# First attention: order of ScalarE's exponentials and copies, and which engine writes the upper halves of queries and keys

## The reference, cut to what matters

```
x = layernorm(x)
q, k, v = x @ Wq, x @ Wk, x @ Wv          # 16 heads of 64 columns
scores  = (q / 8) @ k.T, causal mask
attn    = softmax(scores)
out     = (attn @ v) @ Wo + bo
```

## Time and profile before

| | us |
|---|---|
| median of 3 runs | 3022.37 |
| lowest and highest run | 3019.58, 3025.27 |
| the profiled execution | 3037.7 |
| its span, first to last instruction | 3035.6 |

### The profile page before, as it was taken

The page is one execution under the profiler, slowest core; times in us unless marked ns, Lnnn a source line. Parts: engine busy times, 40 slices in busy tenths (PEclk is TensorE's granted clock), DMA queues, the critical chain, the costliest instruction groups (busy, mean ns, idle before and its releaser), DMA issues.

```text
span 3035.6 us, 54384 instructions
## 1 busy us (share of the span) xinstructions
PE 2616.6 (86%) x20224; PEld 1702.2 (56%) x20224; DVE 2026.0 (67%) x4632; ACT 1685.6 (56%) x3282; POOL 900.1 (30%) x931
## 2 busy tenths in 40 slices
PE   7999999999999999588898558787875969999979
PEld 4666766676667667564446436666765532333325
DVE  5565566556655654257875246999998868888845
ACT  4767566656666665241222227868874436677762
POOL 1000011001100110452232465767876212322221
PEclk9999999999999999799999788898988979999999
DMA  5000000000000001120001111121221540100000
GB/s 184 2 2 2 1 6 6 2 2 6 6 2 2 7 5 42 43 64 14 8 10 54 51 47 49 64 70 64 76 72 56 200 139 2 58 30 30 2 2 29
DMA packets 79941, 114.22 MB, mean 38 GB/s; under 512 B 10109, under 2 KB 48172, under 8 KB 79680
## 3 DMA queue, kind: packets, MB, share of 16 engines
q1 hardware_dynamic: 71488, 97.07, 9.8%
q0 software_dynamic: 8192, 13.67, 1.6%
HBM read 77.66 MB, written 35.78 MB: 37 GB/s over the span
## 4 chain that ended last, share of the span: by engine, by line
PE 27%; issue 13%; POOL 9%; DVE 5%; another core or an unknown queue 3%; ACT 3%; DMA 1%; SPq 0%; POOLq 0%; ACTq 0%; DVEq 0%
POOL arena L2094 7%; PE ps L2323 4%; PE ps L1202 3%; PE ps L1396 3%; PE ps L2294 2%; PE ps L2281 2%; PE ps L2285 2%; ACT arena L2403 2%; PE ps L696 1%; PE ps L1405 1%; PE ps L685 1%; PE ps L1193 1%; DVE Wqkv L2444 1%; POOL arena L993 1%
## 5 line engine op out<-in xcount | busy, mean ns | idle before, releaser
L387 ACT ACTIVATE arena<-ps 128x512 f32<-128x512 f32 (+1 forms) x640 | 334.6, 548 | 376.0 <-PE ps L291 356.2
L499 DVE CUSTOM_DVE_ANT_0 arena<-ps,causal 128x512 f32<-128x512 f32 (+3 forms) x512 | 282.4, 589 | 302.0 <-PE ps L278 266.6
L400 ACT ACTIVATE arena<-arena 128x640 f32<-128x640 f32 (+7 forms) x512 | 394.1, 770 | 37.9 <-DVE arena L499 33.5
L2444 DVE TENSOR_REDUCE Wqkv<-ps 128x2 f32<-128x1024 f32 (+2 forms) x320 | 345.3, 1114 | 87.9 <-PE ps L2285 60.5
L291 PE MATMUL ps<-ident,arena 128*128 128x128 f32 x2304 | 345.9, 282 | 47.6 <-ACT arena L400 30.3
L2094 POOL TENSOR_TENSOR arena<-arena,W 128x1024 f32<-128x1024 f32 x128 | 332.5, 2617 | 134.0 <-DVE W L2046 134.0
L2403 ACT ACTIVATE arena<-ps 128x1024 f32<-128x1024 f32 (+1 forms) x320 | 291.8, 939 | 134.2 <-PE ps L2294 131.2
L1802 PE MATMUL ps<-rope,arena 128*128 128x128 f32 x2048 | 282.6, 300 | 96.2 <-DVE W L2032 47.3
L291 PEld LDWEIGHTS ps<-ident,arena 128*128 128x128 f32 x2304 | 252.0, 142 | 167.7 <-issue 91.2
L577 POOL COPY arena<-arena 128x512 f32<-128x512 f32 x64 | 39.3, 613 | 1027.5 <-DVE arena L523 635.7
L1802 PEld LDWEIGHTS ps<-rope,arena 128*128 128x128 f32 x2048 | 268.2, 213 | 126.3 <-issue 69.1
(11 more groups left out here) (265 smaller groups left out, 4258.4 us busy)
## 6 DMA issues: line engine op xcount, KB each, us to landing
select<-c_rows SPq DMA_DIRECT2D x64, 512.0 KB, 3.6
arena<-q_dram SPq DMA_DIRECT2D x4, 2048.0 KB, 8.9
arena<-k_dram SPq DMA_DIRECT2D x4, 2048.0 KB, 14.0
q_dram<-arena SPq DMA_DIRECT2D x24, 256.0 KB, 3.7
k_dram<-arena SPq DMA_DIRECT2D x24, 256.0 KB, 3.7
arena<-slots_in SPq DMA_DIRECT2D x8, 640.0 KB, 6.7
slots_out<-arena SPq DMA_DIRECT2D x8, 640.0 KB, 4.3
slots_in<-select SPq DMA_DIRECT2D x4, 640.0 KB, 6.4
```

The source lines that it names most:

```text
L387: nc.scalar.activation(k.probT[:, n % 2, b0 * P:(b0 + nb) * P], k.ps[:, 4 + m % 2, 0:nb * P], ACT.Copy)\
L400: nc.scalar.activation(k.prob[:, i % 2, h, 0:w], k.prob[:, i % 2, h, 0:w], ACT.Exp, bias=k.neg_max[:, i % 2, h:h + 1], scale=-1.0, accum_o ...
L499: ins = nc.vector.tensor_tensor_reduce(k.prob[:, i % 2, h, 512 * g:512 * g + w], k.ps[:, banks[h], 0:w], k.causal[:, first:first + w], 1.0 ...
L2444: nc.vector.tensor_reduce(k.least[:, g, As[0]:As[-1] + 1, i % 4, c, :], k.ps[:, 2 * slot:2 * slot + 2, 0:len(As) * w].rearrange("p h (a w) ...
```

## The change

`upper` moves from VectorE's program to ScalarE's. There it stands in steps 0 and 1 of every pair that has a next one (`ahead`), as one activation (Copy with a scale) for each half of 512 columns, waiting for the projection (`qk_ps`) and telling `hi` as before. In steps 0, 1 and 2 of such pairs both exponentials of the step now stand in front of all copies of the step, and in steps 0 and 1 the upper halves stand between the exponentials and the copies. Steps 3 to 7 and the last pair keep their order.

```diff
@@ act_attention_a, pair
+        def upper(w, banks):
+            act.wait_ge(sm["qk_ps"], p * 2 + w + 3)
+            for g in range(2):
+                nc.scalar.activation((k.q_parts, k.k_parts)[w][:, 1 - parity, 0, g * 512:(g + 1) * 512], k.ps[:, banks[g], :],
+                                     ACT.Copy, scale=QK_SCALE[w]).then_inc(sm["hi"], 1)
+
...
             inverse = r is not None and u % 4 == 3
+            if ahead and i < 3:
+                exponential(i, 0)
+                exponential(i, 1)
+            if ahead and i < 2:
+                upper(i, a_banks("project", p, i))
             early = (len(pieces) + inverse + 1) // 2
             for m, b0, nb in pieces[:early]:
                 copy(q, n, m, b0, nb)
             if inverse and early > len(pieces):
                 take_inverse(r, u // 4)
-            if i < 8:
+            if i < 8 and not (ahead and i < 3):
                 exponential(i, 0)
             for m, b0, nb in pieces[early:]:
                 copy(q, n, m, b0, nb)
             if inverse and early <= len(pieces):
                 take_inverse(r, u // 4)
-            if i < 8:
+            if i < 8 and not (ahead and i < 3):
                 exponential(i, 1)
@@ dve_attention_a, pair
-        def upper(w, banks):
-            dve.wait_ge(sm["qk_ps"], p * 2 + w + 3)
-            for g in range(2):
-                nc.vector.tensor_scalar((k.q_parts, k.k_parts)[w][:, 1 - parity, 0, g * 512:(g + 1) * 512],
-                                        k.ps[:, banks[g], :], QK_SCALE[w], None, ALU.mult).then_inc(sm["hi"], 1)
-
...
             if ahead and i < 2:
-                upper(i, a_banks("project", p, i))
                 lower(p + 1, i, 1 - parity, a_banks("project", p, i))
```

## The result

| | before | changed |
|---|---|---|
| median of 22 runs each, us | 3022.98 | 3016.67 |
| lowest, highest | 3017.55, 3030.27 | 3009.41, 3029.24 |
| span of the profiled execution | 3035.6 | 3012.5 |

The ratio is 0.9981, 95% interval 0.9972 to 0.9990: 5.7 us (3.0 to 8.5) faster; the medians differ by 6.3. The two profiled executions differ by 23 us; up to the last pair of the attention they differ by 4 only, so most of the 23 lies behind it, in code that is the same, and isn't counted as an effect of the change. The spans are not used for the verdict; the traces are used for single waits and for pair lengths.

What follows compares the result with a forecast made beforehand. TensorE, busy 1112.6 of 1170 us in the first attention, was taken as the bound, so only its waits count. 8.2 + 3.6 + 0.5 - 5.9 = 6.4 us less gave 3016.0 us, range 3009 to 3023.

Steps and rivals of the forecast that it cites:

- bound of 0.2%: About 6 us on the median, the least a measurement can tell from no change; at 3016.4 us.
- piece 7: TensorE's wait in step 3 for step 2's second exponential: 0.82 us gained in 10 pairs, 0.6 in six.
- piece 24: TensorE start delayed by a later ScalarE copy in step 0: 0.15 us lost in 27 pairs, 0.63 in three.
- piece 10: TensorE work after step 3's exponentials: expected to wait a little, taken up by a later wait.
- piece 25: TensorE work after piece 24: no further loss, its copy being 0.49 us behind.
- Pair 0: First pair, no copies to hide the lower half's wait: projection idles 2.15 us, gain 0.5 us.
- the clock in a rival: Rival of more gained, 18%: a shorter wait in pair 0 may spare 1.2 us of lower clock; 3010 us.
- Copies and inverse in step 1: Step 1's two copies end some 0.3 us later, but their banks are needed a step away: no cost.
- VectorE's relief: VectorE gives up four instructions in each of 31 pairs, 85 us; worth nothing by itself.
- the lower half behind ScalarE: VectorE's lower half waits for a ScalarE result, about 1.95 us after the projection; matters only in pair 0.
- move on: Rival, 8%: piece 7 is freed, but VectorE's maxima of step 3 make later steps give half back; 3022 us.
- Slower: Rival, 5%: step 0's copy ends 0.5 us later than reckoned, piece 24 waits 0.65 in 30 pairs; 3029.5 us.

Runs made afterwards that it cites:

- the order alone: Kernel before, with both exponentials ahead of the copies in steps 0 to 2 and VectorE keeping the upper halves; ratio 0.9962 to the kernel before.
- one activation more: Changed kernel plus one unused ScalarE activation of 472 columns in front of the upper halves of step 0; ratio 1.0032 to the kernel before.
- step 4 alone: Kernel before, with both ScalarE copies of step 4 ahead of its first exponential; ratio 0.9944 to the kernel before.

## Why the prediction was right

The forecast was 6.4 us less, 3016.0; measured were 5.7 us by the ratio and a median of 3016.67. It lay on the bound of 0.2% that the prediction names and came out just inside it, at 0.19%, with an interval that crosses it. The mechanism held: a gain at piece 7, a smaller loss at piece 24, little else. That the total came so close is in part luck, as the sum below shows. Step by step:

- **Piece 7** (11.8 us forecast). The wait of 0.82 is gone in all 16 pairs. In the six that also normalise, 0.6 was taken: with the order alone pair 4, which has the statistics, saves the whole 0.82, and pairs 5, 13 and 21, which have the norm, 0.67. (Pairs 12 and 20, of pair 4's kind, are among the six with scattered rows; they are taken as pair 4.) That makes 4.5 us instead of 3.6. What follows takes up part of it as said: piece 10 waits 0.44 instead of 0.21 there, and piece 12 0.3 instead of 0.6, waits again counted from start to start. Not foreseen: in pairs 11, 19 and 27, taken as free, piece 7 starts 0.75 us after the scores instead of 0.93, another 0.5 us.
- **Piece 24** (5.9 us forecast, at 0.15 and 0.63). Measured 0.15 in 26 pairs, 0.60 in 11, 19 and 27, and 0.49 in pair 2, where ScalarE's last exponential of pair 1 comes later in this kernel. Behind the start of piece 25 another 0.02 to 0.03 are lost in each, which had been put at nothing. With the 6.1 us at piece 24 that is 6.9 us.
- **Pair 0** was the one term badly sized: 0.5 us was taken for the lower half that comes earlier. Pair 0 is 3.17 us shorter, 0.82 of it at piece 7. The projection of step 1 starts 0.57 us earlier (30.25 - 25.98 = 4.27 us after the pair's first scores, before 30.59 - 25.75 = 4.84). That of the values, which also waits for the lower half, starts 2.17 us after the transposes behind that projection instead of 2.78, 0.61 less. So the lower halves are worth 1.18 us, not 0.5. The remaining 1.17 us are the clock's: the four matmuls of the projection take 1.98 us where the earlier trace rows has 3.20, and the transposes behind it start 1.82 us after its start instead of 2.99. That it goes with this part of the change is shown: in all eight profiles of kernels in which ScalarE writes pair 0's upper halves the granted clock is 1.00 from 31 to 41 us, and in all five without it is at 0.65 or 0.66 in one or both of its halves (the order alone has 1.00 in the first and 0.66 in the second). What keeps the clock up is less well shown: the waits around it are shorter (1.58 us against 2.15 at the projection), and that these decide is argued. The forecast had the clock in a rival, at 1.2 us, outside the sum. TensorE there, in the kernel before, then in the changed one:
```profile
33.58 0.63 PE L291 MATMUL ps<-ident,arena 128*128 128x128 f32 x2
...
36.36 2.05 PE L217 MATMUL ps<-Wqkv,XNT 128*128 128x128 f32 x16 [1.34 <-DVE arena L478]
```
```profile
30.25 1.98 PE L211 MATMUL ps<-XNT,arena 128*128 128x512 f32 x4 [1.58 <-DVE arena L489]
32.07 0.38 PE L291 MATMUL ps<-ident,arena 128*128 128x128 f32 x2
...
34.24 2.05 PE L217 MATMUL ps<-Wqkv,XNT 128*128 128x128 f32 x16 [1.20 <-DVE arena L489]
```
- **Steps that were put at nothing.** Copies and inverse in step 1, VectorE's relief, and outside pair 0 the lower half behind ScalarE, cost and gave nothing that the traces show. The multiplication rule of the Trainium skill ("ScalarE: Activation LUTs", Rules for kernel authors) sends this work to VectorE; for this form the trace has it the other way round, 593 ns on ScalarE over 124 instructions against 686 on VectorE in the earlier trace rows. The rule gives its factor of three for bf16, and the source here is f32 in PSUM.
- **The sum.** 8.2 + 4.5 + 2.4 - 6.9 is 8.2 us by the measured sizes, and the six pairs add next to nothing to it (their gains and costs by these sizes cancel within 0.1). In the traces the other 25 save 7.0: pairs 16, 26 and 29 take 1.6 us more than their parts say, for waits of their own, and pairs 1 and 8 take 0.4 less. The forecast sized the savings 2.8 us too low and the cost 1.0 too low. That its 6.4 is so near 5.7 is therefore in part luck: errors of both signs, among them a clock gain that stood outside the sum and small waits in single pairs. The six pairs alone moved by +2.8 and -3.5 us in the two profiles of the changed kernel, and the interval of the result is 3.0 to 8.5.
- **The rivals.** The wait did not move on: with the order alone the common pairs are shorter by the whole 0.82. Slower needed 0.41 us a pair at piece 24; one activation more (0.46 on top of 0.15) shows that side, at 1.0032.

So the change is two things with opposite signs. The order of step 2 saves about 12 us; the upper halves in front of four copies cost about 7 and bring 2 in pair 0.

## What to carry to other kernels

When one engine is busy 95% of a stage, list its own waits by place and price them one at a time; taking 75 us off an engine that is hardly waited for gave nothing outside the first pair, and putting one instruction behind another gave 12. An in-order queue should be ordered by who is waited for next: what TensorE will need soonest goes first, and work whose user is far away (here the upper halves: moved back by 1.4 us, they still kept no projection waiting) goes behind it. A moved instruction that reaches its place exactly when its input is ready has no slack, so count everything that then stands in front of the next one.

## What was not expected

- The long waits for copies, up to 3.2 us, lie in the pairs in which GpSimd scatters, and on the third chip they are missing. The wait list of step 4 alone there has
```profile
PE ps L291 <- ACT arena L387: 0.5, 2, 0.3
```
where the earlier trace rows has 15.4 us in 7. The runs of the kernel before are about 3% shorter on that chip (2929.4 us against 3023 to 3035). What delays ScalarE and VectorE in these pairs on the other chips isn't known; the profile names no releaser it can see ("remote").
- The kernel before scattered over 30 us (3020.51 to 3050.32) in one set of runs, while pair lengths outside the six repeated to 0.02 us. A saving of 0.5 us a pair is read better in one trace than in twelve runs.
